# A windowed-attention kernel whose score and output products move to 64x64 tiles in two shared banks, with the maximum subtracted on GpSimd

## What is computed

```python
def _swin_block(x, shift, mask, ...):          # x: 8 x 56 x 56 x 160, 5 heads of 32, windows of 7 x 7
    sc = x
    x = _ln(x, ln1g, ln1b)
    if shift: x = roll(x, (-3, -3))             # the second block only, with a mask
    q, k, v = split(windows(x) @ qkvw + qkvb)   # 64 windows of 49 tokens in an image
    attn = q @ k.T * 32 ** -0.5 + bias (+ mask) # 49 x 49 for each window and head
    attn = softmax(attn)                        # float32 throughout
    x = sc + unwindow((attn @ v) @ projw + projb)
    h = gelu(_ln(x, ln2g, ln2b) @ w1 + b1) @ w2 + b2
    return x + h
```

## Time and profile before

| what | value |
|---|---|
| median of 3 runs | 3472.59 us |
| profiled execution: its time, its span | 3461.46 us, 3459.9 us |
| PE busy, share of the span | 3252.6 us, 94% |
| PEld / DVE / ACT / POOL busy | 84% / 67% / 53% / 24% |
| mean granted TensorE clock | 0.980 |

### The profile page before, as it was taken

The page is one execution under the profiler, slowest core; times in us unless marked ns, Lnnn a source line. Parts: engine busy times, 40 slices in busy tenths (PEclk is TensorE's granted clock), DMA queues, the critical chain, the costliest instruction groups (busy, mean ns, idle before and its releaser), DMA issues. The chain is left out here.

```text
span 3459.9 us, 93945 instructions
## 1 busy us (share of the span) xinstructions
PE 3252.6 (94%) x35410; PEld 2917.9 (84%) x35410; DVE 2319.8 (67%) x6973; ACT 1835.4 (53%) x4329; POOL 835.7 (24%) x1402
## 2 busy tenths in 40 slices
PE   7996999999999999999999999999999999999689
PEld 6884788888888888888888888888888888888589
DVE  1114777777777777777777777777777777777332
ACT  1112566666666666666665555556555565555221
POOL 5301222222222222222222222222222222222010
PEclk9997999999999999999999999999999999999889
DMA  5321111111111111111211111111111111111275
GB/s 103 94 74 46 26 36 35 35 35 34 30 32 32 35 35 35 35 35 35 52 34 37 30 29 35 35 35 33 32 35 24 35 35 35 35 30 30 47 140 93
DMA packets 246673, 148.29 MB, mean 43 GB/s; under 512 B 31729, under 2 KB 246068, under 8 KB 246586
## 3 DMA queue, kind: packets, MB, share of 16 engines
q1 hardware_dynamic: 244882, 146.95, 18.9%
q0 software_dynamic: 1728, 0.48, 0.1%
HBM read 96.74 MB, written 52.50 MB: 43 GB/s over the span
## 5 line engine op out<-in xcount | busy, mean ns | idle before, releaser
L1427 PE MATMUL rm<-w,ht 128*112 128x160 f32 x4480 | 693.7, 304 | 0.0
L1427 PEld LDWEIGHTS rm<-w,ht 128*112 128x112 f32 x4480 | 608.8, 177 | 28.3 <-ACT ht L1010 12.7
L916 POOL TENSOR_TENSOR rs<-ln_tmp,mhalf 112x4 f32<-112x4 f32 (+1 forms) x128 | 125.5, 980 | 1728.1 <-DVE ln_tmp L1080 1728.1
L1010 ACT ACTIVATE ht<-rm 128x448 f32<-128x448 f32 (+1 forms) x640 | 318.7, 498 | 186.2 <-PE rm L111 180.1
L992 ACT ACTIVATE ot_hi<-ra 128x98 fp32r<-128x98 f32 x512 | 103.1, 258 | 456.2 <-PE ra L1406 456.2
L955 ACT ACTIVATE qm<-ra,qmask 128x392 f32<-128x392 f32 x512 | 258.6, 588 | 12.4 <-PE ra L111 3.3
L111 PE MATMUL rm<-z2t_hi,w_hi 128*128 128x448 f32 (+1 forms) x640 | 251.2, 393 | 2.6 <-DVE z2t_rest L1185 1.1
L1375 PE MATMUL s_ps<-kt,qm 128*49 128x49 f32 x8192 | 241.1, 211 | 0.9 <-DVE sc L1140 0.9
L1375 PEld LDWEIGHTS s_ps<-kt,qm 128*49 128x49 f32 x8192 | 209.1, 126 | 36.3 <-issue 30.9
L111 PE MATMUL rm<-z2t_rest,w_rest 98*128 98x448 f32 (+1 forms) x640 | 220.0, 344 | 0.0
L111 PE MATMUL rm<-z2t_hi,w_lo 128*128 128x448 f32 (+1 forms) x640 | 219.1, 342 | 0.0
(11 more groups left out here) (243 smaller groups left out, 9384.0 us busy)
## 6 DMA issues: line engine op xcount, KB each, us to landing
xa<-xs SPq DMA_DIRECT2D x128, 245.0 KB
xr<-xs SPq DMA_DIRECT2D x128, 245.0 KB
xs<-a_tok SPq DMA_DIRECT2D x8, 1960.0 KB, 9.5
xs<-xo SPq DMA_DIRECT2D x64, 245.0 KB
ys<-yz SPq DMA_DIRECT2D x64, 245.0 KB
c_y<-ys SPq DMA_DIRECT2D x48, 260.0 KB
c_y<-ys SPq DMA_DIRECT2D x16, 280.0 KB
c_taps<-in_f_syn SPq DMA_DIRECT2D x24, 126.0 KB, 5.2
```

What stands on the lines that cost most here:

```text
L916: gp.tensor_tensor(rs[1][:, t0:t0 + nt], ln_tmp[1][5][:, t0:t0 + nt], mhalf[:, 0:nt], ALU.pow).then_inc(s_pow, 1)
L1010: act_(ht[:, f * SN + t0 * TT:f * SN + (t0 + nt) * TT], bank_m(i, lm, use)[:, 0:nt * TT], ACT.Gelu_apprx_tanh).then_inc(m_freed(i, lm, use ...
L1427: last = mm(bank_m(i, lm, use)[0:TT, t * DIM:(t + 1) * DIM], ht[:, c:c + TT], keep.w["w2", lm][:, f * DIM:(f + 1) * DIM], start=(f == 0), ...
```

## The change

The scores and the attention outputs are computed by tiles of at most 64 rows and 64 columns.

- **Scores.** A head pair shares 64 rows; `qm` holds two copies of q (even and odd heads, `qpair`) instead of four, and a product uses 64 rows: heads 0 and 1 from rows 0 to 63, heads 2 and 3 from rows 64 to 127. The fifth head's q and k are laid in both halves by p. The order alternates row halves and output halves. The products of rows 0 to 63 write bank 0 of the two-bank tensor `so`, the others bank 1, in columns 0 to 244.
- **Outputs.** The two windows p have their weights and values in rows 0 to 48 and 64 to 112; each product is 49 x 49 x 33, so there are 20 instead of 10, into columns 256 to 420 of `so`, one bank for each p. No zero rows are needed, so the second evacuation of the values (DVE, L1124) goes. Values are computed for 128 tokens at a time instead of 98 (windows lie 64 columns apart in `z1t`), and q and k over 400 columns instead of 392.
- **Bank sharing.** Since scores and outputs share banks, PE waits before each for the other's reader, with a `nop` in front of each group: `scores(3)` for `outputs(0)` of DVE, `outputs(0)` for three score tiles read, `outputs(1..3)` for all four. `outputs(j)` of PE and `scores(j)` are never next to each other any more.
- **Maximum on POOL.** `scores_less_max` is split: DVE takes the maximum (`scores_max`), POOL subtracts it (`less_max`). In POOL's list `less_max(1)` lies behind `inv_std`, `less_max(2)` and `less_max(3)` behind `repeat_rest(z1)`, and `less_max(0)` of the next strip between `repeat_rest(z2)` and `x1b`.
- **Weights.** `pr` is double, its transposes use `gather` (113 x 113) and all go to `pt_ps`; `weights_out` is one ACT instruction of 113 x 490 instead of two.
- **Lists.** The calls in `body` of PE, ACT and DVE stand in another order, and ring `RA` with them. A window pair (p) is now two windows one below the other side of the strip, so the strips' loads and stores take the rows in another order (same number of transfers and sizes).

In the listings, `so` is the new pair of banks, `pt_ps` the transposed weights, `os` the divided outputs, `ra` the ring, `rm` the MLP's banks, `sm` the scores less their maximum, `pr` the exponentials, `ht` the MLP's inner values. Counts here are of products (two instructions each where both inputs are float32).

**PE, from the end of `mlp_in` to the second `mlp_out` pair, before:**

The diff, cut to the scores, the outputs and the four lists:

```diff
-        s_ps, pt_ps, o_ps = bank("s_ps"), bank("pt_ps"), bank("o_ps")
-        PT4 = HEADS * 2 * VW
+        so = ctx.enter_context(nc.psum_tensor("so", [128, 2 * 512], F32))
+        pt_ps = bank("pt_ps")
...
+            def less_max(j, n_):
+                n = n_ * NG + j + 1
+                pool.wait_ge(s_smax, n)
+                reach(pool, s_exp, n - 2)
+                groups = [[WT, 2 * HEADS], [1, WT]]
+                gp.tensor_tensor(view(sm[j % 2], 0, QP, 0, groups), view(sc, 0, QP, 0, groups),
+                                 view(mx, 0, QP, 0, [[1, 2 * HEADS], [0, WT]]), ALU.subtract).then_inc(s_ssub, 1)
+
             def body(i, la, lm, ln):
                 if ln is not None:
                     inv_std(i + 1)
+                if la is not None:
+                    less_max(1, i)
+                if ln is not None:
                     pool.wait_ge(s_norm[0], i + 2)
                     repeat_rest(z1, s_z[0])
+                if la is not None:
+                    less_max(2, i)
+                    less_max(3, i)
                 if la is not None:
                     for hf, (t0, nt) in enumerate(HALF):
                         pool.wait_ge(s_rs[1], RS_STEPS[1] * (2 * i + hf + 1))
                     for hf in range(2):
                         pool.wait_ge(s_norm[1], 2 * i + hf + 1)
                         repeat_rest(z2, s_z[1], *HALF[hf])
+                if ln is not None:
+                    less_max(0, i + 1)
+                if la is not None:
                     if la == 0:
                         for t in range(ST):
...
-                    for h in range(4):
-                        last = act_(qm[:, h * SN + hf * QH:h * SN + (hf + 1) * QH], bank_a(i, use)[:, 0:QH], ACT.Copy,
-                                    scale=keep.qmask[:, h:h + 1])
+                    for odd in range(2):
+                        last = act_(qm[:, odd * QN + hf * QH:odd * QN + (hf + 1) * QH], bank_a(i, use)[:, 0:QH], ACT.Copy,
...
                 if la is not None:
                     exps(0)
+                    exps(1)
+                if ln is not None:
+                    front_hi(0)
+                if la is not None:
                     weights_out(0)
-                    exps(1)
+                    exps(2)
+                if ln is not None:
+                    front_hi(1)
...
-                def scores_less_max(j, n_):
-                    n = n_ * NG + j + 1
-                    dve.wait_ge(s_sadd, n)
-                    s3 = sc[:].rearrange("q (g k) -> q g k", k=WT)
-                    v.tensor_reduce(mx[:], s3, AX.X, ALU.max).then_inc(s_smax, 1)
-                    dve.wait_ge(s_smax, n)
-                    reach(dve, s_exp, n - 2)
-                    v.tensor_tensor(sm[j % 2][:].rearrange("q (g k) -> q g k", k=WT), s3,
-                                    view(mx, 0, QP, 0, [[1, 2 * HEADS], [0, WT]]), ALU.subtract).then_inc(s_ssub, 1)
+                    v.tensor_tensor(view(sc, 0, QP, 0, [[SX, 2], [1, SX]]), view(so, 0, QP, 0, [[512, 2], [1, SX]]), tab,
+                                    ALU.add).then_inc(s_sadd, 1)
+
+                def scores_max(j, n_):
+                    dve.wait_ge(s_sadd, n_ * NG + j + 1)
+                    v.tensor_reduce(mx[:], sc[:].rearrange("q (g k) -> q g k", k=WT), AX.X, ALU.max).then_inc(s_smax, 1)
...
                 if la is not None:
-                    outputs_lo(1)
-                if ln is not None:
-                    front_lo(0)
-                if la is not None:
-                    outputs(2)
-                if ln is not None:
-                    front_lo(1)
+                    scores_biased(3, i, la)
+                    outputs_lo(0)
                 if lm is not None:
                     mlp_out(3)
                 if la is not None:
+                    outputs(1)
+                    scores_max(3, i)
+                    outputs_lo(1)
+                if lm is not None:
+                    mlp_out(4)
+                if la is not None:
+                    outputs(2)
                     outputs_lo(2)
                     outputs(3)
                 if lm is not None:
-                    mlp_out(4)
+                    mlp_out(5)
                 if la is not None:
                     outputs_lo(3)
...
-                        for p in range(2):
+                    reach(pe, s_od, n * NG + {0: 0, 1: 0, 2: 0, 3: 1}[j])
+                    pe.nop(nofuse=True)
+                    for b in range(HEADS):
+                        for row in range(2):
+                            c0 = row * SX + b * WT
+                            h, p = SLOT.index(c0 // GK), c0 // WT % 2
+                            rows = slice(row * WP, (row + 1) * WP)
                             for w in range(2):
-                                c = (2 * j + w) * GK + p * WT
-                                q = qm[:, h * SN + c:h * SN + c + WT] if h < 4 else q4[:, c:c + WT]
-                                k = (kt if h < 4 else k4)[:, c:c + WT]
-                                last = mm(s_ps[w * WP:w * WP + WT, (2 * h + p) * WT:(2 * h + p + 1) * WT], q, k,
+                                c = j // 2 * QH + w * (4 * WQ) + (2 * (j % 2) + p) * WQ
+                                q = qm[rows, h % 2 * QN + c:h % 2 * QN + c + WT] if h < 4 else q4[rows, c:c + WT]
+                                k = (kt if h < 4 else k4)[rows, c:c + WT]
+                                last = mm(so[w * WP:w * WP + WT, row * 512 + b * WT:row * 512 + (b + 1) * WT], q, k,
                                           start=True, stop=True)
                     last.then_inc(s_sfull, 1)
 
-                    reach(pe, s_od, n)
                     for h in range(HEADS):
-                        o = pt_ps[0:GK, h * QP:(h + 1) * QP] if h < 4 else o_ps[0:GK, PT4:PT4 + QP]
-                        last = tr(o, pr[:, h * GK:(h + 1) * GK], keep.ident[0:QP, 0:QP])
+                        last = tr(pt_ps[:, h * GK:h * GK + QP], pr[j % 2][:, SLOT[h] * 2 * WP:(SLOT[h] + 1) * 2 * WP], gather[:])
                     last.then_inc(s_ptf, 1)
 
                 def outputs(j):
                     pe.wait_ge(s_pte, i * NG + j + 1)
                     pe.wait_ge(*a_freed(i - 1, f"V{j}"))
+                    pe.wait_ge(s_sadd, i * NG + (3 if j == 0 else 4))
+                    reach(pe, s_od, i * NG + j)
+                    pe.nop(nofuse=True)
                     for h in range(HEADS):
-                        for w in range(2):
-                            last = mm(o_ps[w * WP:w * WP + WT, h * 2 * VW:(h + 1) * 2 * VW],
-                                      pt[:, h * QP + w * WP:h * QP + w * WP + WT],
-                                      view(vb, 0, GK, j * VG + (w * HEADS + h) * VW, [[2 * HEADS * VW, 2], [1, VW]]),
-                                      start=True, stop=True)
+                        for p in range(2):
+                            for w in range(2):
+                                last = mm(so[w * WP:w * WP + WT, p * 512 + OC + h * VW:p * 512 + OC + (h + 1) * VW],
+                                          pt[p * WP:p * WP + WT, h * GK + w * WT:h * GK + (w + 1) * WT],
+                                          vb[p * WP:p * WP + WT, j * VJ + (w * HEADS + h) * VW:j * VJ + (w * HEADS + h + 1) * VW],
+                                          start=True, stop=True)
...
                     pe.wait_ge(*t2_freed(i, lm))
                     mlp_in(range(2 * FT))
+                if la is not None:
+                    scores(2, i)
+                if lm is not None:
                     mlp_out(0)
+                if ln is not None:
+                    front_turned(0)
                 if la is not None:
                     weights_turned(0)
-                    scores(2, i)
-                    outputs(0)
...
+                    outputs_turned(0)
+                    scores(3, i)
                 if lm is not None:
                     mlp_out(3)
                 if la is not None:
+                    outputs(1)
+                    weights_turned(2)
+                if ln is not None:
+                    front_product("Q", 0)
+                if la is not None:
+                    outputs_turned(1)
+                if ln is not None:
+                    front_product("K", 0)
+                if la is not None:
+                    outputs(2)
+                    weights_turned(3)
+                if lm is not None:
+                    mlp_out(4)
+                if la is not None:
                     outputs_turned(2)
-                    weights_turned(3)
-                if ln is not None:
-                    front_product("Q", 0)
-                    front_product("K", 0)
+                if ln is not None:
+                    front_product("B", 0)
                 if la is not None:
                     outputs(3)
                 if lm is not None:
-                    mlp_out(4)
+                    mlp_out(5)
                 if la is not None:
```

(2 more changed lines are left out.)

226 lines of the change are left out of this document (104 added, 122 removed).

## The result

The changed kernel takes 3697.56 us (median of 4 runs, 3696.26 to 3701.84), the kernel before 3467.54 in the same comparison (median of 4): a ratio of 1.067, 95% interval 1.065 to 1.070. The prediction was 3628 us, 3510 to 3757, slower with a chance of 0.78. Sign and mechanism came out as written; the measured time lies 70 us above the 3628, and these have a cause that the prediction only named as a way to fail. One of the four runs of before took 10726.62 us and is left out of the ratio.

The account below looks back on a forecast made before the run. The prediction took PE (TensorE) as the bound. Work, chains and vanished waits gave +2.4 us a step in layer 0 and +2.8 in layer 1; 32 x 5.2 = 166 us on 3461.46 made 3628 us, range 3510 to 3757.

Parts of the forecast that it names:

- Work of PE: Sum of PE's own work in one step, waits left out: -1.1 us a step, 70 us in all.
- the scores: PE's score groups: four tiles in one round take 0.46 instead of 0.92 us, -0.46 a tile, -1.84 for four.
- The outputs: PE's attention output groups: 40 smaller instructions take 0.60 instead of 0.71 us, -0.44 for four.
- the values: PE's 32 value matmuls, loading 128 columns instead of 98: +0.8 us a step.
- Chain A: Maximum, POOL's subtraction, x1b, inv_std and normalisation delay the first T1: PE waits 0.7 us in layer 0, 1.9 in layer 1.
- Chain B: From outputs(1) through division, maximum, subtraction and exponential to the third transposed output: PE waits 2.3 us in both layers.
- Chain C: At the projection: mlp_out(5), moved ahead, no longer covers the wait: +1.5 us in layer 0, +0.2 in layer 1.
- Waits that go: Old PE waits on q, on T2 and behind outputs(2)'s weights vanish: -1.0 us in layer 0, -0.5 in layer 1.
- The sum of a step: PE's work, three chains and vanished waits added: +2.4 us a step in layer 0, +2.8 in layer 1.
- Rival 1: Row halves on PE don't overlap; scores stay 0.95 us, outputs rise to 1.06: +2.0 a step, 3756 us; chance 0.16.
- Rival 2: Chains A and B are shorter because ACT and DVE run ahead, 0.3 us each: 3436 us, within 2%; chance 0.13.
- Rival 3: Packed products are PE's gain and nothing is late at the three chains: -118 us, 3343 us; chance 0.09.

Follow-up runs that it names:

- e8_ot3_late: Kernel before, with outputs_turned(3) behind mlp_out(5) on PE and, on DVE, the evacuation mlp_out(5) ahead of outputs_lo(3): 3547.0 us, ratio 1.025.
- e9_abc: Changed kernel, tile 0's subtraction behind x1b, tile 3's maximum and tile 2's division earlier, outputs(3) and outputs_turned(3) moved up in all lists: 3371.1 us, ratio 0.973.
- e10_abc_half: e9_abc with one wait loosened: the first mlp_in group waits only for the evacuation of the first half of z2t_rest: 3353.4 us, ratio 0.969.
- e12_best_rows_apart: e10_abc_half with loops exchanged, so row halves run one behind the other in scores and outputs: 3479.2 us, ratio 1.004.
- e1_x1b_first: Changed kernel, with POOL's subtraction of tile 0 of the next step behind x1b instead of ahead of it: 3573.5 us, ratio 1.031.
- e4_rows_apart: Changed kernel with loops exchanged, so row halves run one behind the other in scores and outputs instead of alternating: 3809.5 us, ratio 1.099.
- e11_sub1_first: Changed kernel, with POOL's subtraction of tile 1 ahead of inv_std instead of right behind it: 3726.8 us, ratio 1.076.
- e2_ot3_first: Changed kernel, with outputs_turned(3) ahead of mlp_out(5) on PE alone: 3767.5 us, ratio 1.086.
- e6: Kernel before, with only the subtraction of the maximum moved from DVE to POOL: 3445.4 us, ratio 0.995.
- e7: Kernel before, with only the values' products loading 128 instead of 98 columns of z1t as weights: 3483.0 us, ratio 1.006.

## Why the prediction was right, and what it missed

**Work of PE.** Predicted -1.1 us a step. In layer 0 the waits of PE went from 1.41 us a step (0.44 for T2, 0.49 for q, 0.30 for the projection, 0.18 for `pt`; the 0.56 of the earlier trace rows is a mean, 0.44 in layer 0 and 0.66 in layer 1) to 4.78 (0.89 + 0.21 + 1.55 + 1.66 + 0.47), while the step grew by 2.18: the work changed by -1.2. In layer 1 the waits went from 0.84 to 4.39, while the step grew by 2.79: the work changed by -0.8. Inside the sum the scores came out as written: from the first to the last start of a group are 0.47 us instead of 0.92, -0.45 where I had -0.46. Up to the next group it is -0.35 where outputs used to follow (0.95 against 0.60) and -0.45 where a group stood alone, which is what the +0.3 for taking them apart was for. The outputs, -0.12 a group, and the values, +0.8, were right.

**Chain A.** Predicted +0.7 and +1.9; waits of 0.92 and 2.17. The timeline of POOL, and of DVE, through the chain:

```profile
1009.23 1.01 POOL L915 TENSOR_TENSOR sm<-sc,mx 113x490 f32<-113x490 f32 x1 [4.26 <-DVE mx L1162]
1010.20 3.46 POOL L941 TENSOR_TENSOR x1b<-x,b 112x160 f32<-112x160 f32 x7
1013.62 0.55 POOL L896 TENSOR_TENSOR ln_tmp<-st 112x7 f32<-112x7 f32 x3
...
1017.03 1.01 POOL L915 TENSOR_TENSOR sm<-sc,mx 113x490 f32<-113x490 f32 x1
1019.86 0.93 POOL L902 TENSOR_TENSOR z<-z,one 112x448 f32<-112x448 f32 x1 [1.82 <-DVE z L1112]
```

```profile
1008.41 0.67 DVE L1162 TENSOR_REDUCE mx<-sc 113x10 f32<-113x490 f32 x1
...
1017.09 2.68 DVE L1112 TENSOR_SCALAR z<-xa,mean,rs 112x160 f32<-112x160 f32 x7 [5.03 <-POOL rs L896]
```

From the start of the maximum, 1008.41, to T1, 1020.92, are 12.5 us, predicted 12.3. Two links were wrong and cancel in part, by luck: `inv_std` up to the normalisation took 3.47 and not 3.96, the normalisation 2.68 and not 2.00. The subtraction took 1.01, predicted 1.05.

**Chain B.** Predicted +2.3; 1.76 in two waits, and 1.8 by its removal. **Chain C.** Predicted +1.5 and +0.2, measured alone +1.38 and +0.23. The places, the engines put down for them and their order were right.

**Waits that go.** -1.0 and -0.5 were taken. The one at T2, the one for q and the 0.18 for `pt` went whole, but 0.47 us came back at `mlp_in`, which leaves -0.64 and -0.37: the score group that stands behind T2 is shorter by 0.45 us, and what it used to hide, the last evacuation of T2, now shows. The prediction asked "what is late next" of the chains and not of the group that got faster.

**The sum of a step.** Predicted +2.4 and +2.8 us, measured +2.18 and +2.79 at full clock. That this is so close is in part luck: chain B was 0.5 us too long, and chain A, the waits that go and, in layer 1, the work were off by 0.1 to 0.4 the other way.

**The step that failed** is the sum of the steps taken for the whole time. Predicted 32 x 5.2 = 166 us, measured 159 in the steps that run at full clock; the other 72 us of the difference are half-speed stretches. The prediction had the condition, "if the granted clock dropped in the steps, as longer waits may let it", and gave it neither a price nor a chance. The waits of up to 1.2 us that it set against a drop stand outside the repeated steps; within them none of the kernel before is over 0.71 us. By e8_ot3_late waits alone bring it on; by e9_abc, e10_abc_half and e12_best_rows_apart packed products with short waits do not. That waits are the cause is shown; which wait brings it on and which doesn't is not, and the length alone does not decide it. In the changed kernel every step of layer 0 has the same wait of 1.66 us at the projection, and in most of the layer two steps are slowed and the third is not. In layer 1, with 2.2 us at T1 in every step, most often four are slowed and the fifth is not: the stretch begins 14.6, 14.9, 15.3 and 15.6 us behind the table load in turn, and then none does. The 1.55 us at `outputs_turned(2)` has no stretch right behind it in that kernel; in e1_x1b_first, where that is the only long wait left in layer 1, 7 of 30 steps are slowed. So the moment at which a wait falls counts too, and what sets it no run asks.

**The rivals.** Rival 1 is out (e4_rows_apart). Its price had a slip: outputs of 1.06 us against the 0.60 of my sum are +1.84 for four groups and not +1.3, so that it comes to about 3796 and not 3756, outside the stated range. In e4_rows_apart they take 0.88. Rival 2, short waits, is out. Rival 3, faster, failed in the lists as written; with chains A, B and C out of the way it is what happens: 3371 us in e9_abc, and 3353 with one wait more loosened in e10_abc_half, against the 3343 that it named.

## What to carry to other kernels

Cost a change of the work and a change of the lists apart: here the same products gave +6.7% in one set of lists and -3.1% in another. When an operation moves to another engine, follow what it is put ahead of in that engine's list, and when one engine's list is changed, change those of all engines that serve the same tile. On a kernel that PE bounds, price every new wait twice: its length, and the slowed stretch that may follow it.

## What was not expected of the hardware

- With four tiles of 64x64 a matmul instruction starts every 12 ns on average (24 in 0.28 us), where with two column halves of 128 rows one started every 24 ns (40 in 0.95 us). The floor of about 25 ns that the Trainium skill gives ("TensorE: Matmul & The Clock Gate", Part 1) is not one for products on different tiles; the trace decides against it. They have to alternate: in row order the same 40 take 0.88 us instead of 0.59.
- DVE's first normalisation takes 1.05 us instead of 0.36 when it starts together with a subtraction of 1.01 us on POOL, and ends 0.10 us behind it (the 0.16 of the expectation for e11_sub1_first is a misreading); its six successors take 0.35. Moving the subtraction restored it (e11_sub1_first). The Trainium skill says that the two engines share a pair of ports and that it is "an exclusive lock (not a bandwidth split)" ("Trainium Architecture — The Big Picture", What this means for kernel authors); the trace agrees.
- The granted clock fell from 1.00 to 0.50 behind waits of PE of 1.3 to 2.5 us in stretches where PE was otherwise busy, nearly always between the last moments of the wait and 2 us after it. In the changed kernel each time cost 1.55 to 1.65 us, about as much as the wait itself; in layer 0 of e2_ot3_first it cost 3.7 to 5.2. In the kernels with no wait over 0.72 us in the steps (before, e6, e7, e9, e10, e12) it never fell in the 62 steps.
